# Graph network of four blocks on one core: heads of the last attention layer in a new order, their outputs packed into full tiles, two of five low halves made by TensorE and ScalarE

## The reference

```
h = (x @ W1).reshape(n, 8, 96);  al_s, al_d = <h, a_src>, <h, a_dst>
e = leaky_relu(al_s[src] + al_d[dst])          # self loops are added
alpha = exp(e - max per dst) / sum per dst
y = elu(segment_sum(alpha * h[src]) + b1)      # 625 x 768, 8 heads side by side
out = the same with W2 (768 x 768), one head of 768 features, b2
```

## Time and profile before

| | us |
|---|---|
| median of 3 timed runs | 1748.78 |
| all three | 1748.78, 1748.90, 1743.21 |
| the profiled execution | 1743.84 |
| its span in the profile | 1742.0 |
| TensorE busy / VectorE / ScalarE / GpSimd | 1521.1 / 846.3 / 588.6 / 529.3 |

### The profile page before, as it was taken

How to read it: one execution, slowest core, us unless ns; L and a number is a source line. 1 busy time by engine, 2 the same in 40 slices (tenths; PEclk the granted TensorE clock), 3 DMA queues, 4 the chain that set the end, 5 groups by cost and what they waited for, 6 DMA issues and landing times.

```text
span 1742.0 us, 26951 instructions
## 1 busy us (share of the span) xinstructions
PE 1521.1 (87%) x10142; PEld 1471.5 (84%) x10142; DVE 846.3 (49%) x2128; ACT 588.6 (34%) x1172; POOL 529.3 (30%) x681
## 2 busy tenths in 40 slices
PE   3978999997879999796999999999999998666777
PEld 3757989997879989786999999999999997566777
DVE  5886776316467753255533313141322225599643
ACT  3334444223344543222322232222232122366421
POOL 3244334232333332233213232323234231222222
PEclk9989999998989999987899999999999999868888
DMA  2222111122211111132112122112132222100012
GB/s 88 84 77 62 35 41 49 53 83 74 77 49 49 45 41 52 56 111 91 32 31 63 45 66 64 50 50 63 41 100 83 74 81 71 51 1 1 10 47 90
DMA packets 88125, 101.64 MB, mean 58 GB/s; under 512 B 9593, under 2 KB 80744, under 8 KB 87997
## 3 DMA queue, kind: packets, MB, share of 16 engines
q1 hardware_dynamic: 71986, 71.20, 14.1%
q10 hardware_dynamic: 16011, 28.73, 5.2%
HBM read 88.12 MB, written 11.78 MB: 57 GB/s over the span
## 4 chain that ended last, share of the span: by engine, by line
PE 60%; DVE 15%; issue 10%; ACT 6%; DMA 5%; POOL 3%; DVEq 1%; ACTq 0%; POOLq 0%; SPq 0%
PE ps L845 37%; PE ps L1025 7%; PE ps L1007 4%; PE ps L911 4%; DVE junk L1872 3%; DVE prob L1920 3%; DMA xl<-x_scratch 2%; PE ps L878 2%; DVE prob L1928 2%; PE ps L1069 2%; PE ps L1046 2%; ACT pairs L1237 1%; DMA xl<-in_x 1%; POOL pairs L1148 1%; DMA stage<-in_W 1%
## 5 line engine op out<-in xcount | busy, mean ns | idle before, releaser
L1148 POOL TENSOR_TENSOR pairs<-stage,pairs 128x256 fp32r<-128x256 f32 (+3 forms) x472 | 372.9, 808 | 791.1 <-ACT pairs L1237 789.8
L845 PE MATMUL ps<-pairs,XB 128*125 128x256 f32 (+2 forms) x2880 | 415.3, 304 | 26.4 <-issue 15.0
L845 PEld LDWEIGHTS ps<-pairs,XB 128*125 128x125 f32 (+1 forms) x2880 | 403.9, 192 | 30.1 <-issue 16.7
L845 PE MATMUL ps<-pairs,XA 128*125 128x256 f32 (+3 forms) x2655 | 374.1, 302 | 6.4 <-DVE XA L1558 2.3
L845 PEld LDWEIGHTS ps<-pairs,XA 128*125 128x125 f32 (+2 forms) x2655 | 368.2, 187 | 8.4 <-issue 2.9
L1237 ACT ACTIVATE pairs<-stage 128x256 fp32r<-128x256 f32 (+3 forms) x472 | 188.6, 423 | 506.0 <-PE ps L845 388.9
L1558 DVE TENSOR_TENSOR Hl<-ps,Hl 125x768 fp32r<-125x768 f32 (+3 forms) x57 | 43.6, 818 | 271.0 <-ACT Hl L1287 271.0
L911 PE MATMUL ps<-AT,Hg 125*128 125x314 f32 (+1 forms) x1080 | 165.7, 313 | 3.8 <-DVE rl L1956 3.8
L911 PEld LDWEIGHTS ps<-AT,Hg 125*128 125x128 f32 (+1 forms) x1080 | 160.7, 189 | 4.8 <-DVE rl L1956 3.7
L1195 POOL TENSOR_SCALAR prob<-prob,rden 125x625 f32<-125x625 f32 x80 | 70.9, 886 | 229.3 <-DVE rden L1936 229.3
L878 PE MATMUL ps<-ident,prob 125*125 125x125 f32 x475 | 85.3, 327 | 49.1 <-POOL prob L1195 18.6
(11 more groups left out here) (215 smaller groups left out, 1708.7 us busy)
## 6 DMA issues: line engine op xcount, KB each, us to landing
stage<-in_W SPq DMA_DIRECT2D x192, 128.0 KB, 2.3
stage<-in_rel SPq DMA_DIRECT2D x99, 192.0 KB, 2.4
stage<-in_root SPq DMA_DIRECT2D x91, 64.0 KB, 1.8
x_scratch<-xo ACTq DMA_DIRECT2D x15, 375.0 KB
xl<-x_scratch ACTq DMA_DIRECT2D x15, 375.0 KB
stage<-in_rel SPq DMA_DIRECT2D x42, 128.0 KB, 2.1
stage<-in_root SPq DMA_DIRECT2D x12, 192.0 KB, 2.4
stage<-in_W SPq DMA_DIRECT2D x12, 192.0 KB, 2.4
```

The lines of the kernel that those rows point to most:

```text
L845: last = mm(o, X[:rows, xi, a, P * (s0 + t):P * (s0 + t) + m], pair(n, b), start=k == 0 and i == 0 and t * pitch % BANK == 0, stop=k == le ...
L1148: nc.gpsimd.tensor_tensor(pair(n, 1), staged(n), pair(n, 0).bitcast(F32), ALU.subtract).then_inc(*up("weights_lo", "weights lo", n))
```

## The change

The list gets a new order for block 3's heads: `elu_sum` moves to the head of its tick, `elu_high` behind `attention_T`. For two of a head's five row tiles (d = 1 and 3) a new step `att_minus`, one tick after `attention_T`, makes the low part in PSUM: TensorE multiplies the high part in SBUF by a matrix of minus one on the diagonal and adds the product to the transposed row in PSUM (two matmuls of 504 and 126 columns), and ScalarE, no longer VectorE, copies the rest to SBUF. The matrix is made at the start by ScalarE from the identity, ahead of its first DMAs. ELU's minimum moves from VectorE to GpSimd in block 3. ELU's high and low parts are made in XA[6] to XA[8] in turn, and one or two DMAs of SP inside SBUF move each head's 96 rows to where they lie in six tiles of 128; the second projection takes those as 6 k-tiles of 128 rows, with weight tiles of 128 x 256. Each aggregation also waits for the copies made by ScalarE.

```diff
+LOW_BY_PE = (1, 3)
@@ gat_steps, l == 3
         for t in range(heads * NT + 3):
             h, d = t // NT, t % NT
+            if h > 1 and d == 2:
+                yield ("elu_sum", l, h - 2, 0)
...
-            if h > 1 and d == 2:
-                yield ("elu_sum", l, h - 2, 0)
+            if t >= 4 and (t - 4) % NT in LOW_BY_PE:
+                yield ("att_minus", l, (t - 4) // NT, (t - 4) % NT)
             if 0 < t <= heads * NT:
                 yield ("softmax", l, (t - 1) // NT, (t - 1) % NT)
-            if h > 1 and d == 2:
-                yield ("elu_high", l, h - 2, 0)
...
             if t >= 3:
                 yield ("attention_T", l, (t - 3) // NT, (t - 3) % NT)
+            if h > 1 and d == 2:
+                yield ("elu_high", l, h - 2, 0)
@@ weight tiles, sources and places
-        rows = 128 if l < 3 else 96
+        rows = 128
-                    return [(XA, k, 96) for k in range(8)]
+                    return [(XA, k, 128) for k in range(6)]
-                return ("x2 lo", s[1], k) if s[1] == 3 else ("x2 lo", s[1], k // 4, k % 4)
+                return ("x2 moved", (128 * k + 127) // 96) if s[1] == 3 else ("x2 lo", s[1], k // 4, k % 4)
-                return XA, h
+                return XA, 6 + h % 3
@@ TensorE
+                elif kind == "att_minus":
+                    q, d = fill_of["attention_T", *s[1:]], s[-1]
+                    pe.wait_ge(*at("minus one"))
+                    pe.wait_ge(*at("att hi", *s[1:]))
+                    for j0, nj in ((0, 4), (4, 1)):
+                        last = mm(slot(q)[:P, 128 * j0:128 * (j0 + nj)].rearrange("p (j c) -> p j c", j=nj)[:, :, :P + 1],
+                                  minus[:P, :P], att_of(*s[1:3])[:P, j0:j0 + nj, 0, P * d - 1:P * d + P],
+                                  start=False, stop=True, skip_group_check=True)
+                    last.then_inc(*up("psum_filled", "filled", *s))
@@ SyncE
+                if s[0] == "elu_high" and s[1] == 3:
+                    h = s[2]
+                    sp.wait_ge(*at("x2 lo", 3, h))
+                    f0 = 96 * h
+                    cut = min(96, 128 - f0 % 128)
+                    for p0, p1 in ((0, cut), (cut, 96)):
+                        if p0 < p1:
+                            r0 = (f0 + p0) % 128
+                            sp.dma_start(XA[r0:r0 + p1 - p0, (f0 + p0) // 128, :, :].bitcast(F32),
+                                         XA[p0:p1, 6 + h % 3, :, :].bitcast(F32)).then_inc(
+                                *up(f"x2_moved{h}", "x2 moved", h, by=16))
@@ GpSimd
+                elif kind == "elu" and s[1] == 3:
+                    n = agg_order[s[1:]]
+                    pool.wait_ge(*at("elu exp", n))
+                    nc.gpsimd.tensor_scalar(mn[:96, n % 2, :], mn[:96, n % 2, :], 1.0, -1.0, ALU.min, ALU.add).then_inc(
+                        *up("elu_min", "elu min", n))
@@ ScalarE
+            act.wait_ge(*at("ident"))
+            A(minus[:, :], ident[:, :], ACT.Copy, scale=-1.0).then_inc(*up("minus_one", "minus one"))
             act.dma_start(b1t[:, :16], I["b1_0"]).then_inc(*up("bias_in", "b1 in", 0, by=16))
...
+                elif kind == "att_minus":
+                    q, d = fill_of["attention_T", *s[1:]], s[-1]
+                    act.wait_ge(*at("filled", *s))
+                    A(att_of(*s[1:3])[:P, 0:NT, 1, P * d:P * d + P], pitched(q, 1), ACT.Copy).then_inc(
+                        *up("att_lo_act", "att lo", *s[1:]))
+                    G.same(("att lo", *s[1:]), "free", q)
...
+                    if l == 3 and h >= 3:
+                        act.wait_ge(*at("x2 moved", h - 3))
@@ VectorE
                 elif kind == "attention_T":
-                    transposed_lo(s, att_of(*s[1:3]), "att")
+                    if not by_pe(s):
+                        transposed_lo(s, att_of(*s[1:3]), "att")
...
+                    if l == 3:
+                        continue
                     dve.wait_ge(*at("elu exp", n))
```

More of the change, by code:

```diff
@@ L507, in build @@
                    "graph_out1", "graph_in", "degrees_out", "degrees_in"]
-                + [f"counts_back{d}" for d in range(NT)] + [f"counts_in{d}" for d in range(NT)])
+                + [f"counts_back{d}" for d in range(NT)] + [f"counts_in{d}" for d in range(NT)] + ["elu_min", "att_lo_act", "minus_one"] + [f"x2_moved{h}" for h in range(GAT_HEADS[3][0])])
         sems = {n: ctx.enter_context(nc.semaphore(n)) for n in names + dmas}
@@ L877, in _ @@
                         m = P + CLONES if kind == "mean_T" and j == NT - 1 else P
[L878 to L879 removed]
+                        o = 128 * j + by_pe(s)
+                        last = mm(slot(q)[:m, o:o + P], M[:, d, P * j:P * j + m], ident[:P, :P], is_transpose=True,
+                                  start=j in (0, 4) or not by_pe(s), stop=True, skip_group_check=True)
+                    last.then_inc(*up("psum_filled", "filled", *s))
[7 more added lines that the diff above has]
+                                  start=False, stop=True, skip_group_check=True)
                     last.then_inc(*up("psum_filled", "filled", *s))
@@ L1667, in _ @@
                 kind = s[0]
-                if kind not in ("mask_rows", "score_rows", "softmax", "attention_T", "aggregate", "elu", "elu_high", "combine", "relation_sum", "part",
+                if kind not in ("mask_rows", "score_rows", "softmax", "attention_T", "aggregate", "elu", "elu_high", "combine", "relation_sum", "part", "att_minus",
                                 "split", "early", "late", "spread", "split_to", "norm_T") or (kind == "attention_T" and s[1] < 3):
```

15 lines of the change are left out of this document (10 added, 5 removed).

## The result

The change makes the kernel slower: 1761.64 us, the median of 6 runs (1759.38 to 1768.27), against 1747.93 for the kernel before on the same chip (6 runs, 1743.21 to 1751.36). The recorded ratio is 1.0095, with a 95% interval of 1.0075 to 1.0115 (the quotient of the two medians is 1.0078). The forecast was 1733.7 us, a gain. The profiled execution took 1762.26 us with a span of 1760.5, 18.5 more than the span before.

A forecast was written before the change was run, and what follows sets the result against it. VectorE was taken to bound the head stage, TensorE the second projection. Terms -10.6 - 4.0 + 0 + 0.5 + 1.5 = -12.6 us gave 1731.2 or 1736.2 by starting time; the middle, 1733.7, was forecast, range 1722 to 1747.

The forecast's parts named there:

- The second projection: Matmuls after the last layer's heads: 90 fewer at 0.118 us each, so 10.6 us less.
- S + 7.9: Last head's move lands 7.9 us after the second projection's start (S, 1644.3 us), before TensorE wants it: no stall.
- New wait 1: Head stage: VectorE waits before the ELU sum for GpSimd's scaling and minimum, 1.8 us a head.
- The scaling kept at 0.79: Head stage: GpSimd's scaling of a row was reckoned at its old duration, 0.79 us.
- VectorE's 12.2 us a head: Head stage: VectorE's busy time falls from 14.16 to 12.2 us without two low halves and the ELU minimum.
- New wait 2: Head stage: VectorE waits for ScalarE's copy of row 2, behind TensorE's product, 0.6 us a head.
- The clock: Head stage: TensorE's longest gap falls to about 2 us, giving full clock for most of the stage.
- Before and behind the five heads: First two heads: 0, from -2 to +2; last two ELUs with the slower minimum: +0.5, from 0 to +2.
- The start: Kernel start: ScalarE copies the identity's negative before issuing x's loads, +1.5 us, between 0 and 2.4.
- Rival 4: Head stage: ScalarE's queue and TensorE lock into a loop at clock 0.50, 18 us a head, 1755 us; chance 0.08.
- the 14.6 forecast: Head stage: one head takes 12.2 + 1.8 + 0.6 = 14.6 us, for 15.5 before.

The follow-up runs named there:

- G: The kernel before with only the packing into six tiles of 128 and its moves: 1734.71 us, ratio 0.9940.
- B: The changed kernel with GpSimd's minimum and add replaced by two multiplications by one, leaving the minimum out: 1746.44 us, ratio 1.0004.
- Q: The changed kernel with VectorE's masked scores behind its low halves waiting by semaphore for GpSimd's scaling of the row before: 1751.59 us, ratio 1.0039.
- F: The changed kernel, minimum still on GpSimd, with all five low halves back on VectorE: 1752.12 us, ratio 1.0052.
- A: The changed kernel with ELU's minimum back on VectorE, all else as changed: 1731.29 us, ratio 0.9926.
- R: As I, but with the old order of steps from the last head on: 1727.42 us, ratio 0.9891.
- I: As A, with the matrix of minus one made behind the issue of x's loads instead of ahead: 1732.23 us, ratio 0.9931.
- J: As I, but with the order of steps of the kernel before: 1730.87 us, ratio 0.9924.
- H: The changed kernel with all low halves and the minimum on VectorE and no matrix of minus one, leaving packing and new order: 1741.06 us, ratio 0.9981.
- P: H with VectorE's masked scores behind a low half waiting by semaphore for GpSimd's scaling of the row before: 1738.03 us, ratio 0.9963.
- E: The kernel before with only ELU's minimum moved to GpSimd: 1754.70 us, ratio 1.0066.
- O: The changed kernel with two filler memsets on VectorE between low half and scores in tick 2: 1762.41 us, ratio 1.0084.

## Why the prediction was wrong, by its steps

- **The second projection, -10.6: right in kind, 1.8 short.** 270 matmuls cost 32.15 us in G, 10.6 less. In the changed kernel TensorE stood 1.64 us after 72 of them, where I had the move landing at S + 7.9. The last move was issued at S + 6.0 instead of 4.5 (the minimum is 1.5 us dearer than I took it), and TensorE went on 4.3 us later, for my 3.4. (Small slips: the 1.5 us fixed are 1.6 by the same rows, and the projection before ends at 1687.0, not 1686.4.) The median move of this size takes 3.8 from issue to landing:
```profile
XA<-XA SPq DMA_DIRECT2D x4, 471.0 KB, 3.8
```
- **New wait 1, the first of two steps that failed.** "The scaling is of the same kind and width, so I take 0.80" for the minimum, between 0.5 and 1.5: it is 2.30. The two are one opcode, and I took the price of the opcode for that of its two operations. Even the upper bound was too low. The wait is 3.25 for 1.8. By B this is about half of the loss.
- **The scaling kept at 0.79, the second step that failed.** Every sum of the prediction takes the scalings and VectorE's rows at the durations of the kernel before; what a new neighbour does to them was put at nothing, without a reason. In the changed kernel two scalings a head take 2.78 and 2.21 us. B has the price of the minimum nearly as forecast and keeps these scalings, at 1746.44 us; Q takes them away with the minimum at its full price, for 10 us.
- **VectorE's 12.2 us a head: 13.2.** This is the same step on VectorE's side. I subtracted the low halves and the minimum and left the others as they were. But a scaling that starts together with the scores instead of beside a low half takes 1.34, and the mask row behind it 1.39 for 0.86; a second mask row takes 1.35 beside a late scaling. So I take the removed low halves for what had kept GpSimd and VectorE apart; F, with all of them back, still has long scalings, so they are not enough. In A one mask row is stretched, and the surplus is 0.5.
- **New wait 2, 0.6: it is 1.9 to 2.9.** I reckoned the product would find TensorE free at 8.1 us. The aggregation ahead of it began late, as the row of the tick was scaled in 2.78 us, and ran at the low clock. The product itself was right (0.52 us at full clock, forecast 0.5). Q takes the long scalings away: wait 2 is gone and a head is 17.0 for 18.9. (TensorE's sum of 9.8 us in the prediction is 10.0 by its own terms, which changes nothing.)
- **The clock.** Full clock was forecast because TensorE's longest gap would be some 2 us. The gap ahead of the ELU sum is 3.7, for 4.47 before, and the clock of the heads, from sum to sum, 0.70 to 0.76. But short gaps don't bring the full clock by themselves. In A TensorE never waits more than 1.0 us for another engine in these heads, and its clock is 0.87 in three and 0.76 in two; in R it is 1.00 in one head and 0.76 in the next:
```profile
1589.58:1603.79 14.21, 11.88 (x64) 11.19 (x64) 13.28 (x28) 11.04 (x23) 4.66 (x6) 0.76 0.12 35
```
```profile
1578.94:1592.89 13.95, 12.02 (x64) 11.33 (x64) 13.28 (x28) 11.07 (x23) 4.67 (x6) 0.76 0.15 36
```
  (The first line is of A, the second of R.) So the reading of the clock from the gap alone isn't borne out, and what decides it here stays open.
- **Before and behind the five heads, 0 and +0.5: +2.4 and +7.9** (the start apart). They are the same stalls, once in the first and twice in the last part; in the sixth and seventh head the new order adds its long scalings even without the minimum (23.2 us in I, 16.9 in J).
- **The start, +1.5: +0.5.** The table load ran ahead of the wait for the identity (0.73 for 7.45), and x was issued at 1.94. In the trace of before the first activation stands at 8.75, right behind the table load, as the prediction says, though the earlier trace rows don't show it.

Rival 4 came nearest, the slower case to which I gave 0.08: ScalarE waiting for a product behind an aggregation at the low clock, "from 17 us a head". It named the loop but not what would start it, and its clock of 0.50 all through is 0.70 to 0.76. A head of 18.9 on average, against the 14.6 forecast, is 4.3 us more: 1.45 in the wait for the minimum, 1.0 in stretched mask rows, the rest in wait 2. Without the minimum on GpSimd the change would have given 1731.3, near the forecast of 1733.7, though with a head of 13.5 to 14.5 and a costlier end than I had worked out; that nearness is partly luck.

Still open is what decides between 0.92 with 0.79 and 0.80 with 2.78 at equal distances in time. ScalarE's work beside the pairs, the wait ahead of the low half and the memory layout (G and H have the same) don't tell the two kinds apart. That the scores, when they don't wait for the scaling, are what stretches it is shown (P, Q); how they get ahead of a scaling that starts first isn't.

## What to carry to other kernels

Don't price an instruction on another engine by its opcode and width: find a row with the same arithmetic operations, and where none exists let the range reach to several times the nearest. Before moving or removing an instruction, ask which instructions it brings side by side on other engines: here GpSimd's scalings grew from 0.79 to 2.78 us beside VectorE's instructions with two SBUF inputs, and semaphore waits of 0.32 us kept the two apart, which gained 10 us. The same edit can change its sign with another: the two lows by TensorE gained 9 us with the minimum on VectorE and cost 7.5 to 9.5 with it on GpSimd, so measure such edits together.

## What the runs showed of the hardware

- GpSimd's minimum with add over 96 x 628 fp32 takes 2.30 us, two multiplies over the same 0.71; VectorE takes 0.46 for the former.
- Beside VectorE's scores and mask row that minimum takes 2.85 (E), and the mask row 1.30 for 0.86.
- A scaling can take 2.78 us for 0.79 although VectorE's instruction with two SBUF inputs starts 0.53 us after it (H), and 2.93 with that start 0.81 us after it (O). When that instruction waits for the scaling by semaphore, it takes 0.79 (P, Q).
- With no wait of TensorE for another engine over 1.0 us (A), the granted clock of a head was still 0.76 to 0.87.
- A move inside SBUF of 471 KB takes 3.8 us from issue to landing, of 314 KB 3.5 and of 157 KB 3.0 (medians of four each, the changed kernel).
